# A two-layer graph network on one core: window 0's one-hots ahead of the branch, and the last 128 rows of x times Wu made in the edge count

## The reference, cut to what matters

```python
out1 = gat_conv(layer_norm(x), src, dst, W1, a_src1, a_dst1, b1, 4, 192)
out2 = gat_conv(out1, src, dst, W2, a_src2, a_dst2, b2, 2, 96)
x = _layernorm(x + (jnp.concatenate([x, out2], axis=-1) @ Wu + bu))
# layer 1: two relational attentions over the three edge types
h = elu(rgat_conv(x, W1, q1, k1, b1, edge_type, 4 heads of 192))
x = _layernorm(x + rgat_conv(h, W2, q2, k2, b2, edge_type, 1 head of 768))
```

## Time and profile before

| what | value |
|---|---|
| median of three runs | 1876.23 us (1874.57 to 1877.85) |
| the profiled execution's own time | 1875.85 us |
| its span | 1874.0 us |
| TensorE busy | 1775.2 us, 95% of the span |
| VectorE busy | 1540.3 us, 82% |
| ScalarE busy | 744.5 us, 40% |
| mean granted TensorE clock | 0.981 |

### The profile page before, as it was taken

One profiled execution on the slowest core, in us unless ns is written; L12 is line 12 of the kernel. 1 busy time (PEld: TensorE's weight loads), 2 busy tenths in 40 slices (PEclk: granted clock), 3 DMA queues, 4 the chain that ended last, 5 costly groups with the idle time before them and its releaser, 6 DMA issues.

```text
span 1874.0 us, 24445 instructions
## 1 busy us (share of the span) xinstructions
PE 1775.2 (95%) x8514; PEld 1337.5 (71%) x8515; DVE 1540.3 (82%) x2913; ACT 744.5 (40%) x1279; POOL 21.9 (1%) x40
## 2 busy tenths in 40 slices
PE   6799977799999999999999999998999989999997
PEld 3544545799654655555999999997999965555554
DVE  7889979999569538999999999996467458998996
ACT  5899979534134221111444444443211222332331
POOL 0000011010000000000000000000000000000000
PEclk8989989899999999999999999998999999999999
DMA  6200159541440447676222221210466567767764
GB/s 187 69 19 27 60 203 388 162 120 31 144 146 12 173 148 251 216 239 188 90 70 75 60 86 58 88 30 30 137 191 208 167 228 255 247 222 250 249 218 162
DMA packets 168068, 276.67 MB, mean 148 GB/s; under 512 B 11819, under 2 KB 132386, under 8 KB 164486
## 3 DMA queue, kind: packets, MB, share of 16 engines
q1 hardware_dynamic: 115942, 212.43, 34.7%
q10 hardware_dynamic: 48736, 48.48, 8.0%
q0 software_dynamic: 3264, 14.16, 2.0%
HBM read 219.31 MB, written 55.71 MB: 147 GB/s over the span
## 4 chain that ended last, share of the span: by engine, by line
PE 83%; DVE 8%; ACT 4%; DMA 3%; issue 2%; ACTq 0%; DVEq 0%; SPq 0%
PE ps L1432 26%; PE ps L1461 17%; PE ps L1379 12%; PE ps L1283 10%; PE ps L1077 4%; PE ps L1094 4%; PE ps L1186 2%; PE ps L1215 2%; PE ps L1334 1%; DVE work L2463 1%; ACT work L1548 1%; DVE work L2457 1%; ACT work L1625 1%; DVE feat L2120 1%; DVE feat L2428 1%
## 5 line engine op out<-in xcount | busy, mean ns | idle before, releaser
L1461 PE MATMUL ps<-work 128*128 128x384 f32 (+1 forms) x784 | 256.7, 486 | 2.4 <-DVE work L2213 2.4
L1432 PE MATMUL ps<-counts,work 128*128 128x193 f32 x1440 | 239.3, 327 | 0.0
L1379 PE MATMUL ps<-work 128*128 128x384 f32 (+1 forms) x720 | 236.4, 489 | 0.0
L1432 PEld LDWEIGHTS ps<-counts,work 128*128 128x128 f32 x1440 | 235.9, 190 | 0.3 <-DVE work L2463 0.3
L1863 ACT ACTIVATE work<-work,s 128x1280 f32<-128x1280 f32 x111 | 151.4, 1364 | 212.0 <-DVE work L2457 210.3
L1461 PEld LDWEIGHTS ps<-work 128*128 128x128 f32 x784 | 148.4, 189 | 107.8 <-DVE work L2213 3.6
L1379 PEld LDWEIGHTS ps<-work 128*128 128x128 f32 x720 | 136.4, 190 | 96.5 <-issue 15.9
L2463 DVE SCALAR_TENSOR_TENSOR work<-work,counts 128x1280 f32<-128x1280 f32 x112 | 166.4, 1486 | 0.1
L2028 DVE TENSOR_SCALAR work<-work,winoff 125x480 bf16<-125x480 f16 x480 | 158.1, 397 | 5.0 <-PE ps L1094 4.8
L1432 PE MATMUL ps<-counts 128*128 128x193 f32 x960 | 160.9, 327 | 1.1 <-ACTq L574 1.1
L1432 PEld LDWEIGHTS ps<-counts 128*128 128x128 f32 x960 | 157.4, 190 | 1.8 <-ACTq L574 1.8
(11 more groups left out here) (301 smaller groups left out, 2602.7 us busy)
## 6 DMA issues: line engine op xcount, KB each, us to landing
work<-hs_d SPq DMA_DIRECT2D x75, 960.0 KB, 5.3
work<-nomask_d SPq DMA_DIRECT2D x70, 320.0 KB, 3.3
work<-pqrow_d SPq DMA_DIRECT2D x12, 1280.0 KB, 6.4
nomask_d<-work SPq DMA_DIRECT2D x40, 320.0 KB, 7.8
hx_d<-work ACTq DMA_DIRECT2D x60, 192.0 KB, 2.7
counts<-hx_d SPq DMA_DIRECT2D x120, 96.0 KB, 1.9
hs_d<-feat ACTq DMA_DIRECT2D x22, 480.0 KB, 3.7
counts<-pqrow_d SPq DMA_DIRECT2D x6, 1280.0 KB, 6.2
```

The lines of the kernel that those rows point to most:

```text
L1379: last = mm(bank(n % 4 if i else n % 2, cols), xT[:, j, t * P:(t + 1) * P], wv[:, j, :], start=(j == 0), stop=(j == DT - 1))
L1432: last = mm(sums_at(c, t, u), xe_of(c)[i % RING][:, t * P:(t + 1) * P], hx[:, i % RING, 0:1 + c.width], start=(r == 0 and k == 0 and t % T ...
L1461: last = mm(bank(product_bank(g, i), width), a[:, at * P:(at + 1) * P], h_block(n, block_, width), start=(m == 0), stop=(m == STEPS_D - 1) ...
```

## The change

Six things are done at once.

1. `groups_sel` is made later, and window 0's one-hots are made by VectorE and ScalarE ahead of their branches. TensorE's program branches where it did.
2. The last tile of x times Wu (t = 9, both halves) is made in the edge count: `u_last_half(0)` behind window 23 and `u_last_half(1)` behind window 25, six matmuls each, into PSUM bank 7. The columns of x are there already (`xT`).
3. Wu's upper rows are loaded for it once more, into `counts[TOTAL]` (`wu_early`), by SyncE after x's columns and the twelfth weight product; GpSimd adds the identity to them.
4. ScalarE copies the two halves out behind its copies of the counts of windows 24 and 26, and sends the tile to `base_d`. `total_counts` waits until that has landed.
5. `ALL_LO` becomes windows 17 to 22: VectorE makes two narrow one-hots of windows 23 to 26 again.
6. In B there are 18 groups instead of 20, and six half groups, behind steps 0, 3, 6, 9, 12 and 15, instead of ten.

```diff
-ALL_LO = range(17, 27)
+ALL_LO = range(17, 23)
-U_GROUPS = 2 * T
+U_GROUPS = 2 * (T - 1)
+U_LAST_AT = (23, 25)
+U_LAST = len(U_LAST_AT)
-U_AFTER_STEP = {i: (U_BEFORE + n // 2, n % 2) for n, i in enumerate([0, 2, 4, 6, 8, 10, 12, 14, 16, 17])}
+U_AFTER_STEP = {i: (U_BEFORE + n // 2, n % 2) for n, i in enumerate([0, 3, 6, 9, 12, 15])}
...
+        wu_early = [flat_f[TOTAL][:, q * DT * 384:(q + 1) * DT * 384].rearrange("p (j c) -> p j c", j=DT) for q in range(2)]
+        u_last = flat_f[TOTAL][:, 2 * DT * 384:2 * DT * 384 + D]
...
+            sp.wait_ge(m_done, 2 * DT)
+            for q in range(2):
+                sp.dma_start(wu_early[q], t_in["Wu"][0:D, q * 384:(q + 1) * 384].rearrange("(j p) c -> p j c", p=P)) \
+                    .then_inc(u_in, 16)
...
+            def own_part(wu):
+                for j in range(DT):
+                    w_ = wu[j // 3][:, j, j % 3 * P:(j % 3 + 1) * P]
+                    last = nc.gpsimd.tensor_tensor(w_, w_, identf[:, :], ALU.add)
+                last.then_inc(u_diag, 1)
+            pool.wait_ge(u_in, 16 * 2)
+            own_part(wu_early)
...
+            def u_last_half(q):
+                if q == 0:
+                    pe.wait_ge(u_diag, 1)
+                    pe.wait_ge(xt_a_in, 16 * DT)
+                    pe.wait_ge(xt_a_zero, 1)
+                    pe.wait_ge(crow_saved, 1)
+                else:
+                    pe.wait_ge(u_ev, 1)
+                for j in range(DT):
+                    last = mm(bank(7, 384), xT[:, j, (T - 1) * P:T * P], wu_early[q][:, j, :], start=(j == 0), stop=(j == DT - 1))
+                last.then_inc(u_mm, 1)
...
                     for n in spread(w, G_WINDOWS, 2 * T):
                         g_unit(n)
+                    if w in U_LAST_AT:
+                        u_last_half(U_LAST_AT.index(w))
...
+            def u_last_fetch(q):
+                act.wait_ge(u_mm, q + 1)
+                nc.scalar.activation(u_last[:, q * 384:(q + 1) * 384], bank(7, 384), ACT.Copy).then_inc(u_ev, 1)
+                if q:
+                    act.wait_ge(u_ev, 2)
+                    act.dma_start(base_d[(T - 1) * P:T * P, :], u_last).then_inc(u_out[0], 16)
...
             extras = act.value_load(tab[0:1, NW:NW + 1], min_val=0, max_val=MAXG)
+            first_c0 = first_chunk(0)
             act.wait_ge(keys_ready, 1)
+            one_hot_lo(0, 0, 1, 1, OH, c0=first_c0)
             with act.If(extras < 1):
-                one_hot_lo(0, 0, 1, 1, OH)
...
-            link(v.tensor_tensor(groups_sel[:, :], identf[0:96, 0:8], identf[0:96, 32:40], ALU.add))
-            v.tensor_tensor(groups_sel[:, :], groups_sel[:, :], identf[0:96, 64:72], ALU.add).then_inc(keys_ready, 1)
...
                 dve.wait_ge(m_done, 2 * DT)
+                dve.wait_ge(*u_left(T - 1))
...
+            first_c0 = ahead
+            window(0, 0, SLOW, first_c0, ALO)
+            link(v.tensor_tensor(groups_sel[:, :], identf[0:96, 0:8], identf[0:96, 32:40], ALU.add))
+            v.tensor_tensor(groups_sel[:, :], groups_sel[:, :], identf[0:96, 64:72], ALU.add)
```

More of the change, by code:

```diff
@@ L941, in _ @@
             end_phase(pool, 0)
-            pool.wait_ge(u_in, 16 * 2)
-            for j in range(DT):
-                w_ = wu_half[j // 3][:, j, j % 3 * P:(j % 3 + 1) * P]
-                last = nc.gpsimd.tensor_tensor(w_, w_, identf[:, :], ALU.add)
-            last.then_inc(u_diag, 1)
+            pool.wait_ge(u_in, 16 * 4)
+            own_part(wu_half)
             end_phase(pool, 1)
@@ L1119, in _ @@
                     m_unit(i)
+                for q in range(2):
+                    u_last_half(q)
                 for n in range(2 * T):
@@ L1542, in _, with first_chunk, one_hot_lo @@
             act.sem_inc(win_saved, BANKS)
-            def one_hot_lo(u, w, free, made, slots, n_lo=ALO):
-                c0 = act.value_load(tab[0:1, bass.ds(w + TAB_C0, 1)], min_val=0, max_val=NCH - WCH)
+            def first_chunk(w):
+                return act.value_load(tab[0:1, bass.ds(w + TAB_C0, 1)], min_val=0, max_val=NCH - WCH)
+            def one_hot_lo(u, w, free, made, slots, n_lo=ALO, c0=None):
+                if c0 is None:
+                    c0 = first_chunk(w)
                 act.wait_ge(oh_used, free)
@@ L1592, in _ @@
                     m_unit(i)
+                for q in range(2):
+                    u_last_fetch(q)
                 deviations()
@@ L2081, in _, with extra_chunks @@
                 n_link[0] = links
-                with dve.Fori(0, NW // SLOW) as it:
+                def extra_chunks(w, c0):
+                    e0 = dve.value_load(tab[0:1, bass.ds(w, 1)], min_val=0, max_val=MAXG)
+                    e1 = dve.value_load(tab[0:1, bass.ds(w + 1, 1)], min_val=0, max_val=MAXG)
+                    with dve.If(e0 < e1):
+                        with dve.Fori(e0, e1) as e:
+                            ch = nc.s_assert_within(
+                                e - e0 + c0 + WCH, 0, NCH - 1, skip_runtime_bounds_check_because=
+                                "a window's chunks end with the last chunk at most")
+                            dve.wait_ge(extra_used, e + 1)
+                            one_hot_lo(OH * WCH, ch)
+                            one_hot_hi(OH * WCH, w, ch).then_inc(extra_ready, 1)
+                extra_chunks(0, first_c0)
+                for w in range(1, SLOW):
+                    c0 = first_chunk(w)
+                    window(w, w, SLOW, c0, ALO)
+                    extra_chunks(w, c0)
+                with dve.Fori(1, NW // SLOW) as it:
                     for u in range(SLOW):
@@ L2086, in _ @@
                         window(w, u, SLOW, c0, ALO)
-                        e0 = dve.value_load(tab[0:1, bass.ds(w, 1)], min_val=0, max_val=MAXG)
-                        e1 = dve.value_load(tab[0:1, bass.ds(w + 1, 1)], min_val=0, max_val=MAXG)
-                        with dve.If(e0 < e1):
-                            with dve.Fori(e0, e1) as e:
-                                ch = nc.s_assert_within(
-                                    e - e0 + c0 + WCH, 0, NCH - 1, skip_runtime_bounds_check_because=
-                                    "a window's chunks end with the last chunk at most")
-                                dve.wait_ge(extra_used, e + 1)
-                                one_hot_lo(OH * WCH, ch)
-                                one_hot_hi(OH * WCH, w, ch).then_inc(extra_ready, 1)
+                        extra_chunks(w, c0)
                 for t in range(T):
```

41 lines of the change are left out of this document (25 added, 16 removed).

## The result

Six runs of the changed kernel gave 1880.53 to 1889.2 us, median 1883.07; six of the kernel before beside them 1873.97 to 1878.76, median 1876.75. The ratio is 1.0033 (95% interval 1.002 to 1.0046): slower by 6.3 us where no change was forecast, and outside the range. The profiled execution took 1883.22 us, its span is 1881.2, 7.2 more than before's 1874.0, at a mean granted clock of 0.982.

What follows compares the result with a forecast made beforehand. It took TensorE's own work, 83% of the span, as the bound. B -3.1, edge count +3.4 and start -0.2 gave +0.1 us, so 1876.3 us, no change, range 1871.5 to 1880.2.

Steps and rivals of the forecast that it cites:

- the sum itself: Whole kernel: B -3.1, edge count +3.4 and start -0.2 make +0.1 us, so no change.
- its B term, -3.1: Second attention: 2.9 us gained in the steps and 0.2 at the end, though 7.75 us of matmuls leave.
- The two other terms: The terms for B, forecast at -3.1 us, and for the edge count, forecast at +3.4 us.
- The edge count: The moved tile's two halves add 3.4 us net there, one or two records slow; bounds 0 and +6.9.
- The rival with a clock that stays low: Edge count: clock low through the first half and beyond, +6.9 to +9.9 us there, 1881 us in all; chance 0.12.
- not -2.9: B's steps: step 19 ends at 609.0 instead of about 611.96, so 2.9 us come back.
- not -0.2: B's end: the phase ends on ScalarE's copy instead of the last tile's landing, 0.2 us gained.
- The round: B: the ring of three buffers ties VectorE and TensorE to 9.15 us for three steps.
- The first rival: B gives what TensorE's sum says, 7.5 us, for a time of about 1871.7 us; chance 0.12.
- The start: ScalarE's earlier one-hots bring the first weight product 0.2 us earlier; bounds -1.4 and +0.5.
- ready in time: Edge count: GpSimd's six additions are done between 86 and 95 us, needed at 98.7, so free.
- the prediction's estimate by the port lock: Edge count: each GpSimd addition could hold up one VectorE operation by 0.4 us, 2.5 in all, within the slack.

Runs made afterwards that it cites:

- e9: Kernel before with 100 never-run operations added to VectorE's branch for extra chunks; ratio 1.0023 to the kernel before.
- e17: Kernel before with 49 never-run transposes added to TensorE's branch for extra chunks; ratio 1.0034 to the kernel before.
- after: The changed kernel itself, with all six parts of the change, against the kernel before; median 1883.07 us, ratio 1.0033.
- e10: Changed kernel without 27 VectorE waits already covered by earlier ones, so its jump lands at 1844 instead of 1871; the time did not fall.
- e1: Changed kernel with the start put back as before, the moved tile kept; 0.26% slower than the kernel before.
- e2: Kernel before with the new start alone, nothing moved from the second attention; ratio 1.0001 to the kernel before.
- e3: Kernel before with 51 never-run one-element memsets added to VectorE's branch for extra chunks; cost nothing against the kernel before.
- e6: Changed kernel with single matmuls behind each of B's steps 0 to 17 instead of half groups behind every third step; 1878.99 us.
- e8: Changed kernel with the tile's halves behind windows 20 and 22 and single matmuls behind each of B's steps 0 to 17; 1876.6 us.
- e18: Changed kernel moving only the tile's first half, behind window 20, with single products in B and 27 covered VectorE waits left out; 1873.1 us, ratio 0.9985.
- e12: Kernel before, nothing moved out of B, its 30 matmuls placed one or two behind steps 0 to 17; B stayed at 62.5 us.
- e4: Changed kernel with GpSimd's first three weight loads held until VectorE has made its first mask; ratio 1.0035 to the kernel before.

## Why the prediction was wrong

*The step that failed is the sum itself: -3.1 + 3.4 - 0.2 had no term for where the instructions stand, and its B term, -3.1, was twice too large.* The prediction listed what is removed, added and moved, and counted only instructions that run. The tile's halves stand in both sides of the branch, and the start's part unrolls a window into the side never taken. That moved VectorE's landing place from 1792 to 1871 and lengthened its jump from 167 to 229, and it moved TensorE's program by 102. Behind the jump each of the two now waits for a packet of its own instructions: 5.4 us more at VectorE's first mask, and a stop at TensorE that this hides in part. Each alone, in the kernel before and with no work moved, costs most or all of what the change lost, by their ratios: e9 4.3 us (its interval 1.7 to 7.1), e17 6.4 us (3.9 to 8.8). That they share one stage, and cover each other, is shown by after, e10 and e1. No rival of the prediction held this mechanism either. The two other terms do not carry the forecast of no change either: as measured in the profile, -1.5 and +3.7, they come to +2 us without any of these waits.

*The edge count* was right: 3.97 us at the second product of rows and 3.65 at the end against +3.4, with one or two slow records. Against e2, e3 and e17, whose counts end 1.7 to 1.9 us before that profile of the kernel before, it is 5.4. The rival with a clock that stays low did not come: it was up by 100 us.

*B* was mis-sized: -0.9 in the steps, not -2.9, and -0.6 at the end, not -0.2. The round was drawn rightly (chain through VectorE and the ring), but the step behind TensorE's idle time takes 2.39 us where 2.15 was put in, and the exponents before it 1.55, not 1.46, with 0.07 between engines: 9.52 for 9.15, which in five rounds is 1.9 of the 2.0 us that are missing. The phase did end on ScalarE's copy (621.00 + 1.24). The first rival, TensorE's sum of 7.5 us, was nearly reached in another grain: e6 and e8 with single matmuls gained 6.7 us in the steps.

*The start*: -0.2 forecast, +0.08 at the first weight product, 1.0001 in e2; inside its bounds, and no gain. Its price lay elsewhere: e1, without it, has VectorE's landing place at 1817 and no gap.

*GpSimd* was ready in time: six additions of 0.42 us each, done at 86.00 and needed at 99.25. No VectorE operation beside them shows in the chain: VectorE stood idle for 2.52 us until 85.51, and its one-hots from there took 2.21 us instead of 1.98, where the prediction's estimate by the port lock was up to 2.5 us in all.

```profile
83.49 2.51 POOL L957 TENSOR_TENSOR counts<-counts,identf 128x128 f32<-128x128 f32 x6 [11.11 <-DMA counts<-in_Wu]
```

What stays open: why VectorE's gap begins between T 1846 and 1871, since no run crosses that stretch with the place of the landing or the length of the jump alone, and no multiple of 256 lies there; how the losses of the two engines add in medians (after has both and 6.3 us, e17 one and 6.4); and the changed kernel with both waits removed and nothing else, which was not run. e18, which has neither, moves only half of the tile.

## What to carry to other kernels

Code that never runs has a place too: when an edit changes the length of a program ahead of a jump, look at the idle time "issue" behind it in the new trace and at the packets of kind "instruction" in the DMA view, and count each engine's instructions to see which place moved. Work that fills the idle time of a ring of buffers should come in pieces smaller than the idle time of one step: with 18 instead of 30 matmuls of x times Wu the steps were 0.9 us shorter in lumps of three and 6.7 one by one, while 30 one by one gave nothing (e12). A late first result in the stage of masks reached its end about whole: a stop of 4.26 us in e1 became 4.1 from the first mask to A's first exponents, 4.49 in e17 became 5.7.

## What the runs showed of the hardware

The wait at the jump is shorter where the DMA engines are idle: 3.08 us in e4 at a DMA share of 0.11, 6.27 in after at 1.02, 5.68 to 6.84 in the others with the same place. It ends 1.7 to 1.8 us behind the landing of an 8 KB packet of instructions, and TensorE's stop 1.3 to 1.5 us behind that of a 16 KB one. On VectorE a jump over 220 instructions to place 1846 cost 0.83 us and one over 229 to place 1871 cost 6.27. On TensorE it is the place: moving its program by 98 instead of 102 moved the stop by two transposes, four instructions, so that it stayed at instruction 3071. That instructions come in blocks is the Trainium skill's rule (page "Runtime: NRT & Kernel Launch", section "Instruction fetch mechanics"). TensorE's traces agree with it: 12 x 256 is 3072, and the kernel before has 70 packets of 16 KB for the some 17900 instructions that TensorE's program holds without the jumped ones, which by an estimate makes 64 bytes an instruction and 256 a packet. VectorE's 8 KB packets and its place between 1846 and 1871 do not show such a block.
